# Sixteen units of lead for the row maxima of an attention kernel, in place of twelve

## The reference

```python
q = split_heads(_tlin(x, w_q, s_q, b_q))      # the same for k and v
scores = jnp.einsum('bhqd,bhkd->bhqk', q, k) / jnp.sqrt(jnp.float32(HEAD))
attn = jax.nn.softmax(scores, axis=-1)
ctx = jnp.einsum('bhqk,bhkd->bhqd', attn, v)
x = _layernorm(x + _tlin(ctx, w_o, s_o, b_o))
h = jax.nn.silu(fp4_linear(x, w_gate)) * fp4_linear(x, w_up)
x = _layernorm(x + fp4_linear(h, w_down))
```

## Time and profile before

| what | us |
|---|---|
| median of 3 runs | 1953.62 (1952.57 to 1954.31) |
| the profiled execution | 1955.24 |
| its span | 1953.4 |
| PE busy | 1922.9 (98%) |
| DVE busy | 1828.6 (94%) |
| ACT busy | 1641.7 (84%) |
| POOL busy | 918.3 (47%) |
| exponentials, line 1115, 2048 of them | 1086.1 |
| maxima read bank by bank, line 1154, 1470 of them | 901.2 |
| maxima read whole, line 1149, 245 of them | 296.3 |
| maxima read in the projections, line 615, 44 of them | 53.6 |

### The profile page before, as it was taken

How to read it: one execution, slowest core, us unless ns; L and a number is a source line. 1 busy time by engine, 2 the same in 40 slices (tenths; PEclk the granted TensorE clock), 3 DMA queues, 4 the chain that set the end, 5 groups by cost and what they waited for, 6 DMA issues and landing times.

```text
span 1953.4 us, 43156 instructions
## 1 busy us (share of the span) xinstructions
PE 1922.9 (98%) x15934; PEld 1112.8 (57%) x15934; DVE 1828.6 (94%) x3087; ACT 1641.7 (84%) x3225; POOL 918.3 (47%) x779
## 2 busy tenths in 40 slices
PE   8999999999999999999999999999999999999998
PEld 7776444444444444444444444444478888888876
DVE  4799999999999999999999999998299999999997
ACT  6655999999999999999999999998867777777776
POOL 3000446675776665365122122212156666666785
PEclk9999999999999999999999999999999999999999
DMA  7985633444354445435434543542111111111200
GB/s 225 303 262 211 116 56 47 84 89 106 77 106 90 90 94 100 95 78 103 96 85 94 101 95 78 103 96 85 40 36 49 49 50 49 49 50 55 66 30 28
DMA packets 127199, 181.47 MB, mean 93 GB/s; under 512 B 37836, under 2 KB 82636, under 8 KB 126988
## 3 DMA queue, kind: packets, MB, share of 16 engines
q1 hardware_dynamic: 119308, 171.10, 36.8%
q10 hardware_dynamic: 7392, 7.34, 1.2%
q0 software_dynamic: 288, 0.27, 0.1%
HBM read 103.68 MB, written 73.40 MB: 91 GB/s over the span
## 4 chain that ended last, share of the span: by engine, by line
DVE 63%; PE 33%; issue 2%; ACT 1%; DMA 0%; DVEq 0%; SPq 0%; POOLq 0%; POOL 0%; ACTq 0%
DVE halfmax L1154 43%; DVE halfmax L1149 14%; PE ps L1430 10%; PE ps L1469 6%; PE ps L505 4%; PE ps L517 2%; PE ps L1418 2%; PE ps L1441 2%; PE ps L1064 2%; PE ps L1030 1%; PE ps L492 1%; PE ps L1477 1%; DVE room L1620 1%; PE ps L476 1%; PE ps L1486 1%
## 5 line engine op out<-in xcount | busy, mean ns | idle before, releaser
L1115 ACT ACTIVATE room<-ps 128x512 f32<-128x512 f32 x2048 | 1086.1, 599 | 106.4 <-PE ps L1030 80.4
L1154 DVE TENSOR_REDUCE halfmax<-ps 128x1 f32<-128x512 f32 x1470 | 901.2, 678 | 0.0
L1030 PE MATMUL ps<-qs,ks 50*128 50x512 f32 x2048 | 718.9, 449 | 2.6 <-DVE halfmax L1154 1.2
L1005 PE MATMUL ps<-ks,qs 48*128 48x512 f32 x1960 | 678.7, 439 | 4.8
L1064 PE MATMUL ps<-room,vals 128*17 128x256 f32 (+2 forms) x8192 | 578.7, 384 | 0.2 <-ACT craw L1123 0.2
L1005 PEld LDWEIGHTS ps<-ks,qs 48*128 48x128 f32 x1960 | 311.4, 184 | 407.0 <-DVE halfmax L1154 250.0
L1030 PEld LDWEIGHTS ps<-qs,ks 50*128 50x128 f32 x2048 | 325.1, 184 | 19.9 <-ACT room L1115 14.1
L1064 PEld LDWEIGHTS ps<-room,vals 128*17 128x17 f32 x8192 | 167.5, 96 | 251.4 <-issue 187.9
L1149 DVE TENSOR_REDUCE halfmax<-ps 128x2 f32<-128x1024 f32 x245 | 296.3, 1209 | 0.9 <-PE ps L1005 0.8
L164 POOL CAST mrow<-turned_rows 128x32 fp32r<-128x32 f32 x32 | 6.7, 210 | 576.0 <-DVE turned_rows L159 576.0
L1430 PE MATMUL ps<-wguT,xqT 128*128 128x512 f32 (+1 forms) x1152 | 266.8, 384 | 3.9 <-DVE xqT L1660 3.9
(11 more groups left out here) (120 smaller groups left out, 2266.6 us busy)
## 6 DMA issues: line engine op xcount, KB each, us to landing
qk_parts<-parts SPq DMA_DIRECT2D x64, 512.0 KB, 5.4
qs<-qk_parts SPq DMA_DIRECT2D x192, 128.0 KB, 4.3
ks<-qk_parts SPq DMA_DIRECT2D x192, 128.0 KB, 6.7
ctx_raw<-craw SPq DMA_DIRECT2D x64, 256.0 KB
ready<-passing SPq DMA_DIRECT2D x27, 512.0 KB, 4.8
pairs<-ready SPq DMA_DIRECT2D x27, 512.0 KB
out_dram<-fin SPq DMA_DIRECT2D x64, 128.0 KB, 1.9
xin<-in_L_attn_x_dram ACTq DMA_DIRECT2D x14, 512.0 KB, 6.8
```

The lines of the kernel that those rows point to most:

```text
L1005: nc.tensor.matmul(ps[:, MX + max_number(i, u, bank) % 4, :], qs[rows, i.slot(RING), pair, t * P:(t + 1) * P], ks[rows, i.slot(RING), pair ...
L1030: nc.tensor.matmul(ps[:, score_bank(i, s, n), :], ks[rows, slot, pair, kt * P:(kt + 1) * P], qs[rows, slot, pair, qh * BANK:(qh + 1) * BAN ...
L1115: nc.scalar.activation(prob[:, prob_slot(i, s), score_order(i, s)[n], :], ps[:, score_bank(i, s, n), :], ACT.Exp, scale=float(D) ** -0.5). ...
L1154: nc.vector.tensor_reduce(halfmax[:, i.slot(2), bank, column:column + 1], ps[:, at + bank, :], AX.X, ALU.max, negate=True).then_inc(max_re ...
```

## The change

`AHEAD` becomes 8, and with it `LEAD` 16 and `BARE` 488. The maxima's turn moves from step 10 of a group to step 8. The projections make 48 units: chunk 5 has places 1 to 3 in place of 2 and 3, chunks 13, 14 and 15 have place 4 too. Group 0's last unit is now at place 2 of chunk 12, and place 3 there makes the first unit of group 1.

```diff
-AHEAD = 6
+AHEAD = 8
...
-    LONGER = (MAX_FROM + 1, MAX_FROM + 2)
+    LONGER = (MAX_FROM + 1, MAX_FROM + 2, TURN, TURN + 1, TURN + 2)
...
-            places = range(MAX_PER // 2 if k == MAX_FROM else 0, MAX_PER + (k in LONGER))
+            places = range(1 if k == MAX_FROM else 0, MAX_PER + (k in LONGER))
```

## The result

The changed kernel took 1965.53 us (median of 6 runs, 1963.82 to 1968.20), the kernel before 1953.80 beside it: a ratio of 1.0063, with a 95% interval of 1.0051 to 1.0076. That is 11.7 us more; 9.3 were forecast (1962.9), and the range reached to 1966.5. The profiled execution took 1964.86 us and its span is 1963.1, 9.7 above the span before.

The account below looks back on a forecast made before the run. PE was taken to set the pace in the projections, VectorE in attention, ScalarE in steps without maxima. Terms 0.63+0.6+2.1+2.5-4.7+3.9+4.3 summed to +9.3 us, giving 1962.9 us, range 1957.8 to 1966.5.

Parts of the forecast that it names:

- (a): Chunk 5 of the projections: one more unit costs +0.63 us, and PE waiting for group 0's stack +0.6.
- (b): Chunks 13 and 14 of the projections: a fifth unit costs 0.98 to 1.15 us each, +2.1 in all.
- (c): End of chunk 15: the fifth unit's read queues on VectorE and delays the first score, +2.5 us.
- (e): Turn in attention: transposition directly after whole_max exposes its result, 0.13 us at each of 30 turns, +3.9 us.
- (d): Attention: 976 units instead of 980, an eighth of a group less for VectorE, -4.7 us.
- (f): End of attention: two more steps without maxima, +4.3 us, bounds 4.1 and 4.78.
- (h): Clock at the seams: half-clock cost of about 2.2 us kept at the second, no fall at the first.
- rival B: First seam: the clock falls there too after PE's longer wait, total +11.5 us, 1965.1; chance 0.17.
- Rival C: Attention: stacks come late for a group's first unit; 0.3 us over 30 groups is +9, 1972; chance 0.04.
- Rival D: Attention: longer lead ends hidden waits of scores for transposed maxima; with 0.5 a group, 1947.4 us; chance 0.03.

Follow-up runs that it names:

- e6: Kernel before with a lead of seven: 14 units of group 1 in the projections, turn at step 9; 1956.05 us, ratio 1.0018.
- e1: Changed kernel with the transposition one unit later, behind the next unit's first reduction; 1961.95 us, ratio 1.0043 to the kernel before.
- e4: Kernel before, lead of six kept, with the transposition directly behind whole_max, ahead of the second bank's reduction; 1956.67 us, ratio 1.0017.
- e2: Changed kernel with 16 unread matmuls filling PE's wait at the first seam; 1963.25 us, ratio 1.0048 to the kernel before.
- e3: Changed kernel with the fifth unit of chunk 15 made in chunk 8 instead; 1965.32 us, ratio 1.0059 to the kernel before.
- e7: Kernel before with a lead of five: 10 units of group 1 in the projections, no chunk with five units; 1954.40 us, ratio 1.0002.
- e8: Kernel before with a lead of four, 8 units of group 1 in the projections, transposition one unit after whole_max, third-stage parts later; 2045.75 us, ratio 1.0469.
- e5: Kernel before with four more units in the projections, their results made once more in attention; 1961.48 us, ratio 1.0041.

## Why the prediction was right, and where its sum was short

**The direction and the terms held.** (a): a third unit in chunk 5 costs 0.66, forecast 0.63. The 0.6 for the wait on the stack was not there in the changed kernel's profile, whose early chunks ran 1.3 us ahead, but was 0.83 in e6's: it depends on when the first chunks run. (b): 0.98 for chunk 13 and 1.07 for chunk 14, with 2.1 forecast for both. (c): 192.66 to 195.17 is 2.5 us, as worked out from the earlier trace rows; the 0.41 us that the first unit of chunk 15 waits was not forecast. The whole stage came to 5.7 where 5.8 stood, and that close only by luck: the missing 0.6 of (a) and the unforeseen 0.4 in chunk 15 nearly cancel. (e): 0.13 a turn, from a pair of rows that the trace of before had only once; e1 and e4 show it from both sides. By the Trainium skill, "VectorE: DVE Perf Modes", section "The DRAIN you can't avoid", the wait would cost nothing; for this pair the measured period of 38.08 us says otherwise, and it decides. (d) and (f): for the two more steps without maxima the profiles of e2 and e4, neither with a low clock there, give 52.03 against 47.31 us from the last transposition to the last block of scores, so +4.7; forecast was +4.3, so this term was short by 0.4. Its two steps without filler did take 2.14 and 1.98, the 4.1 of the earlier trace rows; most of the rest is that the second step after the last maxima took 2.93 in e2 and 2.45 in e4. The upper bound of 4.78 came from a slip: from 1365.09 to 1405.75 there are 18 steps and not 17, so the average step is 2.26 us and two are 4.5, less than was measured. The stretch from first score to last transposition in e2, without a low clock at its start, is 1357.76 - 193.69 = 1164.07 us, 1.0 less than before; the forecast for (d) and (e) was -0.8.

**What was mis-sized is (h), the clock.** The prediction took it as it stood in one profile: one fall at the second seam kept, none at the first, the latter with a chance of 0.17 as rival B. Rival B's event came: behind the first seam the clock was at half for 6.8 us, and the stretch to the first transposition, 24.95 us, was 2.4 longer than e2's 22.57 with a full clock; forecast was 2.2. That price was low by the same slip: with steps of 2.26 the three blocks at the second seam give 9.36 - 6.78 = 2.6, and 49.90 against e4's 47.31 us from the last transposition on is 2.6 too. B's reasoning isn't borne out either. It tied the fall to the new wait of 2 us, and e3, e4, e6, e7 and e8 have the fall without that wait; whether the wait makes it likelier isn't known. What fails is the step that one profiled execution gives the clock of a kernel: the one of before happened to have no fall where most profiles have one. And the measured 1965.5 lies in the stated range only because the range took in B's price: without those 2.2 us it would end at 1964.3.

**How much the clock is of the 11.7.** Every run lists its mean granted clock, to 0.001. Over the 98 runs of the kernel before and all kernels but e8, with one level for each kernel and one slope for all, a loss of 0.001 goes with 1.06 us (0.54 us for each microsecond of clock withheld), and the runs scatter about that by 1.0 us. The levels at a full clock are, in us (differences taken before rounding):

| kernel | level at clock 1.000 | above before | mean clock | runs |
|---|---|---|---|---|
| before | 1951.4 | | 0.998 | 38 |
| changed | 1960.8 | +9.3 | 0.995 | 6 |
| e1, turn covered | 1957.0 | +5.5 | 0.995 | 5 |
| e2, seam filled | 1960.4 | +9.0 | 0.997 | 6 |
| e3, unit moved | 1960.6 | +9.2 | 0.996 | 5 |
| e4, lead six, bare turn | 1955.6 | +4.2 | 0.999 | 11 |
| e5, units only | 1958.0 | +6.6 | 0.997 | 5 |
| e6, lead seven | 1953.2 | +1.8 | 0.997 | 11 |
| e7, lead five | 1949.9 | -1.5 | 0.996 | 11 |

By this column the change costs 9.3 us at a full clock, with a standard error of 0.5, and the profiles gave 9.4; the forecast's sum was 9.3. The other 2 to 3 us go with the lower clock of its runs. How much exactly is less sure than the column looks, for the slope is an average. The two kinds of e2's runs give about 1.5 us for 0.001, and so do the falls in the profiles: 6.8 us at half clock, 0.0017 of the whole, cost 2.4 to 2.9 us. With 1.5 for all runs the column would say +8.1 for the changed kernel and leave 4 us to the clock. The expectations of e6 (+1.7) and e7 (-2.1) are nearly met in this column. That of e3 isn't: its trace takes 1.4 us off the stage, so it should stand at +7.9, and the column says +9.2. The difference of two such levels has a standard error of 0.6 us, and this one is twice that; it stays open, like the 0.8 of e5.

**What stays open.** Why some kernels lose more clock than others isn't settled. It isn't the lead: e7 with five loses as much as e3 with eight, and e5 with the lead of six loses more than e4 with the same. It isn't PE's idling at the first seam alone, as e3 and the two kinds of runs of e2 show. In the profiles falls come at four places (behind either seam, among the last steps of attention, and at the start of the third stage) and once more at the very end of the program, and which of the four come differs from profile to profile.

Rival C, stacks that come late, didn't occur for any group in attention. Rival D had nothing to win: VectorE was busy for 1140.29 of 1141.49 us.

## What to carry to other kernels

Work taken off an engine that sets the pace only pays if it goes where something is idle, and if the time that it leaves is not filled by the next engine. Here it went from VectorE in attention to a PE that was busy throughout the projections, and the two steps so shortened came back as steps set by ScalarE. A lead between two engines needs to cover the chain between them and no more (here 6.3 us from the transposition to the first score, where four steps of lead leave 4.9 and five leave 7.5), and a change of it shifts where rare instructions meet the regular ones, so look at which instruction stands between a result and its first reader.

For differences of some tenths of a per cent, read the granted clock of every run beside its time before explaining a rest, and don't take the clock's falls from a single profile. What precedes the changed part, here the first chunks, moves by up to 2.8 us between executions as well, so compare stretches between points that both traces have.

## What the runs showed of the hardware

- VectorE starts an independent instruction 0.10 us after one of 0.18, and a dependent one 0.21 to 0.23 after it. In a queue that is hardly ever empty (1140.29 of 1141.49 us busy) this small difference counts in full, some 3.6 us over 30 turns.
- The granted clock fell from the 2.4 to the 1.2 GHz level although PE had idled only 0.21 and 0.45 us in the 7 us before (e3, e4), and stayed up in the kernel before with the same two gaps. A stretch of 6.8 us at half clock cost 2.4 to 2.9 us at the start of attention and 2.6 at the second seam. The Trainium skill, "TensorE: Matmul & The Clock Gate", section "HAM oscillation", ties such falls to long waits for data; in e8 most of them follow waits for a DMA, though of 1.3 to 1.8 us only, and at the first seam they came without one.
- The kernel before varied by 5.7 us over the 38 runs beside the experiments (1951.37 to 1957.07). By the fit half of the clock withheld appears as time, by the falls in the profiles about 0.7 of it (2.4 us for 3.4).
